# Attention of two layers on one core: the first unit of a pair's row maxima is computed one pair earlier, among the weighing of the values

## The reference

```python
q = (xq @ Wq).reshape(B, N, HEADS, D_HEAD)
k = (xc @ Wk).reshape(B, S, HEADS, D_HEAD)
v = (xc @ Wv).reshape(B, S, HEADS, D_HEAD)
scores = jnp.einsum('bnhd,bshd->bhns', q, k) * scale
attn = jax.nn.softmax(scores, axis=-1)
out = jnp.einsum('bhns,bshd->bnhd', attn, v).reshape(B, N, HEADS * D_HEAD)
return out @ Wo + bo
```

## Time and profile before

| what | value |
|---|---|
| median of the runs | 460.51 us (460.4 to 461.62, 3 runs) |
| the profiled execution, its own time | 461.69 us |
| its span, first to last instruction | 459.9 us |
| TensorE busy | 440.5 us, 96% of the span |
| VectorE, ScalarE, GpSimd busy | 60%, 52%, 47% |
| granted clock of TensorE | full from step 0 of the attention on |

### The profile page before, as it was taken

One profiled execution on the slowest core, in us unless ns is written; L12 is line 12 of the kernel. 1 busy time (PEld: TensorE's weight loads), 2 busy tenths in 40 slices (PEclk: granted clock), 3 DMA queues, 4 the chain that ended last, 5 costly groups with the idle time before them and its releaser, 6 DMA issues.

```text
span 459.9 us, 7026 instructions
## 1 busy us (share of the span) xinstructions
PE 440.5 (96%) x2758; PEld 261.3 (57%) x2758; DVE 277.9 (60%) x510; ACT 239.3 (52%) x324; POOL 214.8 (47%) x186
## 2 busy tenths in 40 slices
PE   7998898899999999999999999999999999999896
PEld 4644454565645656655545765545575554754696
DVE  2766636576864586457656848447735677553753
ACT  3853564455557366556445526456416665237632
POOL 4587101026883796444566636873226444255010
PEclk9998999999999999999999999999999999999999
DMA  8600000000000100000001010020001000000000
GB/s 235 226 1 2 1 1 0 0 1 1 0 1 0 36 1 0 0 1 1 1 1 46 2 34 1 2 68 1 0 9 40 0 2 1 1 1 1 0 19 29
DMA packets 7985, 8.89 MB, mean 19 GB/s; under 512 B 561, under 2 KB 6129, under 8 KB 7953
## 3 DMA queue, kind: packets, MB, share of 16 engines
q1 hardware_dynamic: 7952, 8.45, 6.0%
HBM read 7.92 MB, written 0.52 MB: 18 GB/s over the span
## 4 chain that ended last, share of the span: by engine, by line
PE 85%; DVE 7%; ACT 5%; issue 2%; DMA 1%; SPq 0%; DVEq 0%
PE PV L744 18%; PE ST L715 15%; PE ST L637 11%; PE M L688 7%; PE ST L717 5%; PE M L792 5%; PE DEN L759 3%; ACT PT L1301 2%; PE ST L653 2%; PE ST L529 2%; PE M L834 2%; DVE maxw L1499 1%; PE ST L355 1%; PE DEN L482 1%; PE ST L677 1%
## 5 line engine op out<-in xcount | busy, mean ns | idle before, releaser
L1144 POOL TENSOR_TENSOR psums<-PT 128x1024 f32<-128x1024 f32 (+1 forms) x32 | 76.1, 2379 | 132.1 <-ACT PT L1301 131.9
L1301 ACT ACTIVATE PT<-ST 128x1024 f32<-128x1024 f32 (+1 forms) x96 | 98.1, 1025 | 37.7 <-PE ST L717 36.1
L715 PE MATMUL ST<-R 64*128 64x512 f32 (+1 forms) x576 | 104.9, 405 | 0.0
L1641 DVE TENSOR_REDUCE maxw<-M 128x1 f32<-128x512 f32 x128 | 83.5, 687 | 33.1 <-PE M L688 32.8
L744 PE MATMUL PV<-PT,V 128*64 128x512 f32 (+1 forms) x384 | 89.5, 601 | 0.0
L1148 POOL TENSOR_TENSOR psums<-psums,PT 128x1024 f32<-128x1024 f32 x32 | 76.0, 2374 | 2.5
L688 PE MATMUL M<-R 64*128 64x512 f32 (+1 forms) x256 | 71.1, 361 | 0.9 <-DVE AT L1525 0.4
L715 PEld LDWEIGHTS ST<-R 64*128 64x128 f32 (+1 forms) x576 | 57.6, 171 | 14.1 <-ACT PT L1301 8.2
L688 PEld LDWEIGHTS M<-R 64*128 64x128 f32 x256 | 37.0, 184 | 36.1 <-issue 25.2
L744 PEld LDWEIGHTS PV<-PT,V 128*64 128x64 f32 (+1 forms) x384 | 24.7, 136 | 53.4 <-issue 51.1
L1309 ACT ACTIVATE AT<-PV 128x512 f32<-128x512 f32 x32 | 19.1, 598 | 62.3 <-PE PV L744 62.3
(11 more groups left out here) (246 smaller groups left out, 662.0 us busy)
## 6 DMA issues: line engine op xcount, KB each, us to landing
Wo<-in_wo SPq DMA_DIRECT2D x2, 512.0 KB, 6.3
xnT<-in_xT SPq DMA_DIRECT2D x2, 256.0 KB, 3.5
psums<-in_sel SPq DMA_DIRECT2D x1, 512.0 KB, 6.6
X<-in_x SPq DMA_DIRECT2D x1, 512.0 KB, 7.9
w<-in_w SPq DMA_DIRECT2D x2, 256.0 KB, 8.0
PT<-in_wq SPq DMA_DIRECT2D x1, 512.0 KB, 8.7
PT<-in_wk SPq DMA_DIRECT2D x1, 512.0 KB, 8.4
PT<-in_wv SPq DMA_DIRECT2D x1, 512.0 KB, 7.8
```

The source lines that it names most:

```text
L715: return pe.matmul(u[0:ph.KC, h, :], R[head(h), g % 3, part_k, 1, k], R[head(h), g % 3, part_q, 0, :], start=(n == 0), stop=False)
L1144: ins = pool.tensor_tensor(s, p[:, 0], p[:, 1], ALU.add)
L1301: act.activation(PT1[0:ph.KC, g % 2, c], bank(("st", g, c))[0:ph.KC, :, :], ACT.Exp, scale=HD ** -0.5).then_inc(ph.exp, 1)
L1641: ins = dve.tensor_reduce(maxw[:, g % 2, 0, at:at + 1], m[:, :], AX, ALU.max, negate=True)
```

## The change

A function `units_ahead(g)` names the maxima units of pair g that are computed one step earlier. It gives unit 0 for eleven pairs, 2, 4, 5, 7 to 13 and 15, and nothing for the others. For these pairs TensorE issues unit 0 (two products) between unit 1 and unit 2 of the weighing of pair g - 2. The units 1, 2 and 3 stand beside the scores' units 0, 1 and 2 of pair g - 1, and the scores' unit 3 stands alone. The steps in whose weighing something is inserted are then 0, 2, 3, 5 to 11 and 13, and the scores with one unit fewer are those of pairs 1, 3, 4, 6 to 12 and 14.

```diff
+        def units_ahead(g):
+            return (0,) if 2 <= g < NPAIR and g - 2 not in (1, 4, PAIRS + 4) else ()
...
                 elif g + 1 == NPAIR:
                     beside = {0: (0, (0, 0)), 2: (1, (0, 0))}
+                elif units_ahead(g + 1):
+                    beside = {0: (1, (0, 3)), 1: (2, (1, 3)), 2: (3, (2, 4))}
                 else:
                     beside = {0: (0, (0, 3)), 1: (1, (1, 3)), 2: (2, (2, 4)), 3: (3, (2, 4))}
...
                     for c in range(pair(g)[0].units):
                         weigh(g, c)
+                        if c == 1:
+                            for k in units_ahead(g + 2):
+                                scores_max(g + 2, k)
...
                         for k in maxima_units(g + 1):
-                            maxima(g + 1, k)
+                            if k not in units_ahead(g + 1):
+                                maxima(g + 1, k)
...
                     if g == 28:
                         residual(2, 0)
+                    for k in units_ahead(g + 2):
+                        maxima(g + 2, k)
```

## The result

The changed kernel takes 467.56 us (median of 4, 466.96 to 467.83), the kernel before, run beside it, 461.06 us. The ratio is 1.0135, 95% interval 1.0113 to 1.0157: slower by 6.5 us. Forecast were 466.9 us and 6.4 us more.

What follows compares the result with a forecast made beforehand. TensorE's own program was taken as the bound. Seven plain steps (2.5 us), step 3 (0.56) and steps 5, 8 and 13 (1.30, 1.03, 1.05) add 6.4 us to 460.51, giving 466.9 us; 463.5 to 469.5 us for 8 in 10.

Steps and rivals of the forecast that it cites:

- What bounds the kernel: Whole kernel: TensorE is busy for 96% of the span, so only lengthening or shortening its own program counts.
- The gain of 0.22 us a pair: Scores of eleven pairs: one slot fewer, end set by the third exponential, 5.12 us instead of 5.34.
- The insertion at 0.58 us: Eleven weighings: inserted slot 0.23 us, way in 0.21, way back 0.14, together 0.58 us.
- the way in: Weighing, change of shape into the inserted slot: 0.10 us more before it and 0.11 in its first slot, 0.21 us.
- the way back: Weighing, return from the inserted slot to its own shape: 0.14 us, read from the change from denominators to weighing.
- Rival 1: Weighing: changes of shape are hidden, an insertion costs 0.23 us, given back by 0.22; 464.2 us; chance 12%.
- rival 2: Inserted unit: heads run one behind the other, or restarts cost another load, 0.81 us each; 468.8 us; chance 13%.
- Step 3 at 0.56 us: Weighing of step 3: 0.36 us plus a 0.20 us wait for ScalarE, late by a table load.
- Steps 5, 8 and 13 at 1.30, 1.03 and 1.05 us: Scores after VectorE's late side work: first product waits for unit 0's first reduction, 0.73 us after that starts.
- Rival 3: Scores: VectorE's reductions, not the bank loop, space the units; gain 0.86 us a pair, 457.4 us; chance 6%.
- The sum: Whole kernel: 2.5 + 0.56 + 1.30 + 1.03 + 1.05 = 6.4 us slower, 466.9 us on the median.
- the plain seven: Steps 0, 2, 6, 7, 9, 10 and 11, where nothing waits: 0.36 us each, 2.5 us together.

Runs made afterwards that it cites:

- e3: The change with unit 0's maxima of the eleven pairs left out, product and reduction; 0.9947 of the kernel before, 2.39 us less in the self attention.
- e4: The kernel before plus, in the eleven weighings, one slot of two unread 64 x 128 products; 1.0151 of the kernel before, 6.44 us more in the self attention.
- e5: As e4, but the two inserted products have the weighing's own shape and type and 128 columns; 1.0070 of the kernel before, 2.68 us more in the self attention.
- e1: The change without the insertions in steps 3, 5, 8 and 13, seven remaining; 1.0068 of the kernel before, 2.68 us more in the self attention.
- e2: The change with insertions in steps 5, 8 and 13 only; 1.0075 of the kernel before, 3.63 us more in the self attention.
- e6: The change with the maxima products at the fourth and fifth place of each scores unit; 1.0159 of the kernel before, 5.66 us more in the self attention.
- e8: The kernel before with the third scores unit's maxima at places 1 and 3, not 2 and 4, except in pairs 6 and 14; 460.31 us, ratio 0.9968.

## Why the prediction was right

- **What bounds the kernel**: TensorE's own program. Right; what was added to it between the marks appeared in the medians, and e3's came off, to within about a microsecond that the rest of the program adds or takes.
- **The gain of 0.22 us a pair**: right in cause and in the sum, with some luck. e3 measured 2.39 us for eleven, with the end of the scores set by the third exponential. The prediction took a hand-over of 0.05 us everywhere. In the change the product behind the scores starts 0.05 us after the third exponential's end in pairs 1, 4, 9, 10 and 11, but 0.14 to 0.15 us after it in pairs 3, 6, 7, 8, 12 and 14, where it waits for a second semaphore (last section). So the end of the scores moved by only 0.12 to 0.17 us in five of these six. In e3 steps 3 and 12 got the rest in the next phase, steps 7, 8 and 14 stayed at 0.15 to 0.18 us, and pair 6, whose reductions had been late, made up for it with 0.28 us.
- **The insertion at 0.58 us**: right, 0.58 in each plain weighing, 0.59 in e4. Of its parts the way in (0.10 and 0.11) and the slot were read off rows 2 and 5, and the way back, chosen at 0.14 between 0 and 0.19, is 0.15: the next slot of the weighing starts 0.43 us behind the inserted one, and its first slot is 0.05 us long. Rival 1 is refuted by e4 against e5, rival 2 by the one row of both heads.
- **Step 3 at 0.56 us**: 0.55, the change's sum less e1's and e2's; the wait of 0.20 us is in the row above.
- **Steps 5, 8 and 13 at 1.30, 1.03 and 1.05 us**: measured together 3.63 us (e2) against 3.38. The mechanism is shown by the three rows of L693 and by e6. The size was a little low: I took 0.73 us from a reduction's start to the scores', and it is 0.83. The product at 173.57 in rows 6 waits for one semaphore and starts 0.05 us after the reduction's end; the first product of the changed scores waits for two, and starts 0.15 us after it. In step 8 this didn't show, since the first reduction itself began 0.1 us earlier after the weighing's start (4.01 us, before 4.11).
- **Rival 3**, that the reductions space out the scores, is false as put, but not empty: e8 found 0.15 us a pair that a hole in VectorE's reductions did cost. The prediction read the loop over two banks as the whole explanation of the short waits. It explains the units' distance, and the reduction explains the last product's 0.1 us.
- **The sum**: 6.4 us against 6.5 in the times and 6.86 between the marks. By steps the plain seven make 2.7 us (2.5 forecast), step 3 0.60 (0.56), and the late three 3.54 (3.38). The span grew by 5.8 us only, because the profiled execution of before spent 1.1 us more ahead of step 0's weighing than that of the change (104.16 and 103.07). The granted clock shows why, first before, then the change (as above: stretch; us, busy of PE, PEld, DVE, ACT, POOL; granted clock; DMA):

```profile
43.00:46.00 3.00, 3.00 (x13) 1.00 (x6) 1.89 (x5) 0.00 (x0) 0.05 (x1) 0.50 0.00 0
```

```profile
43.00:46.00 3.00, 2.44 (x18) 0.96 (x12) 1.91 (x5) 0.27 (x1) 0.00 (x0) 1.00 0.00 0
```

  TensorE was at its lower level, 1.2 GHz, for these three microseconds in the execution of before, and the 1.1 us arise there. It was right to go by the median, and not by that execution's 461.69 us.

## What to carry to other kernels

In this kernel TensorE streamed without a wait in the weighing, and there work moved into the stream cost its own time plus the change of shape on both sides; it wasn't filled into a hole. Before moving an instruction up in one engine's queue, look at when its buffer will be freed by the other engine: a product that used to be first in a phase with a free bank became one that waits for a reduction, and the whole phase stood behind it. Take the end of a phase apart by the start of the next instruction, and name each of the waits that ends there, and count the semaphores of the instruction that waits; the cheap gain here was in a place number, not in a moved unit.

## What the runs showed of the hardware

- One slot of two products of 64 x 128 in the midst of slots of 128 x 64 costs 0.58 us, of which its own stream is 0.23; two products of 128 columns in the weighing's own shape and type cost 0.22 us for a stream of 0.21 us (e5). The type changed together with the shape, except in one way out of the denominators, where the shape alone went with 0.1 us. The Trainium skill, "TensorEngine Tiling (Array Packing)", Key Properties, says that changing the tiling mode drains TensorE; that agrees, and the price here is 0.35 us for going out and coming back.
- The product behind the scores starts 0.05 us after the exponential that it waits for where that is its only semaphore (234.99 to 235.04 in the scores of pair 10). In the scores of pair 8 it waits for a second semaphore too (that of a DMA, long fulfilled), and starts 0.14 us after the exponential's end:

```profile
206.50 2.06 ACT L1311 ACTIVATE PT<-ST 128x1024 f32<-128x1024 f32 x2 [0.26 <-PE ST L722]
```

```profile
207.67 1.05 PE L658 MATMUL ST<-w,ctxT 96*77 96x512 f32 x2 [0.20 <-ACT PT L1311]
```

  The exponential ends at 206.50 + 1.03 = 207.53. The two values, 0.05 and 0.14 to 0.15 us, part the eleven pairs without an exception: one semaphore in pairs 1, 4, 9, 10 and 11, two or more in pairs 3, 6, 7, 8, 12 and 14, where TensorE's queue has an instruction of its own that only waits. The first products of the scores behind the late reductions show the same 0.15 us. That the second wait is the cause was not tried alone.
- TensorE's granted clock fell to its lower level for a few microseconds in some executions and not in others, though what went before looks alike: in the tail in e1 and e6, at a cost of 1.6 us (40.2 instead of 38.6 us), and ahead of step 0 in the execution of before, at a cost of 1.1 us. What decides it stays open.
- L1614, 128 x 512, took 2.65 us in step 5 where other operations of VectorE on as many elements take 0.69. It is what makes step 5 the dearest. The record holds a strong hint: the same instruction took 0.69 us at 80.99, where GpSimd was idle. In step 5 GpSimd's adding up of the exponentials ran beside it, until 167.56 + 4.82 = 172.38:

```profile
167.56 4.82 POOL L1148 TENSOR_TENSOR psums<-psums,PT 128x1024 f32<-128x1024 f32 x2
```

  L1614 ended 0.53 us after that. In step 13 it took 2.18 us and ended 0.55 us after GpSimd's instruction, which ended at 283.34. So it looks as if L1614 waits for GpSimd's instruction to end; no run here moved one of the two to try it.
